# Score sums of a gated layer kept in two PSUM tiles, with V's columns cleared by ScalarE

## The reference, cut to what matters

```python
Q = einsum('bshd,hde->bshe', layernorm(x), Wh)
K = einsum('bshd,hde->bshe', ctx, Wh)
V = einsum('bshd,hde->bshe', ctx, Wh)
scores = einsum('bshe,bthe->bhst', Q, K) / sqrt(128)
A = maximum(abs((scores * Dn).sum(axis=0)), 1.0)   # one A for the whole batch
O = einsum('hst,bthe->bshe', A, V)
Y = (O - mean) / sqrt(var + eps) * gamma + beta
x = x + tanh(g0) * ((relu(layernorm(x) @ wg) * Y) @ wo)
```

## Time and profile before

| | |
|---|---|
| time, median of 3 runs | 1507.49 us (1504.81 to 1509.27) |
| the profiled execution's own time | 1504.33 us |
| its span | 1502.5 us |
| TensorE busy | 1483.4 us (99%) |
| VectorE busy | 1096.5 us (73%) |
| ScalarE busy | 698.3 us (46%) |
| GpSimd busy | 744.9 us (50%) |
| mean granted TensorE clock | 0.999 |

### The profile page before, as it was taken

How to read it: one execution, slowest core, us unless ns; L and a number is a source line. 1 busy time by engine, 2 the same in 40 slices (tenths; PEclk the granted TensorE clock), 3 DMA queues, 4 the chain that set the end, 5 groups by cost and what they waited for, 6 DMA issues and landing times.

```text
span 1502.5 us, 20476 instructions
## 1 busy us (share of the span) xinstructions
PE 1483.4 (99%) x7182; PEld 1246.3 (83%) x7182; DVE 1096.5 (73%) x1592; ACT 698.3 (46%) x1094; POOL 744.9 (50%) x774
## 2 busy tenths in 40 slices
PE   7999999999999999999999999999999999999998
PEld 5888888888888887888888888888888888888887
DVE  7776778788578687677686763777778778778672
ACT  4444434445565545555646534344344344443442
POOL 5556666771445553545645534137237137237236
PEclk9999999999999999999999999999999999999999
DMA  6888788876778779888898785373473562562422
GB/s 225 301 262 271 262 282 282 255 234 221 250 229 279 237 221 305 261 246 282 240 288 281 209 240 158 116 217 105 125 212 107 144 208 95 146 199 93 149 90 85
DMA packets 237753, 316.05 MB, mean 210 GB/s; under 512 B 135696, under 2 KB 161680, under 8 KB 237456
## 3 DMA queue, kind: packets, MB, share of 16 engines
q1 hardware_dynamic: 237648, 314.71, 66.0%
HBM read 210.32 MB, written 117.31 MB: 218 GB/s over the span
## 4 chain that ended last, share of the span: by engine, by line
PE 86%; DVE 4%; DMA 3%; POOL 2%; SPq 1%; ACT 1%; issue 1%; DVEq 0%; ACTq 0%; POOLq 0%
PE ps L1785 33%; PE po L1785 10%; PE pyb L1664 8%; PE ptb L1785 7%; PE pyb L1785 7%; PE ps L1699 5%; PE po L1664 5%; PE pyb L1769 3%; PE ptb L1769 3%; PE pyb L1773 2%; PE ptb L1773 1%; PE ptb L1669 1%; PE ps L1664 1%; DMA wy_scratch<-misc 1%; POOL reg L1536 1%
## 5 line engine op out<-in xcount | busy, mean ns | idle before, releaser
L1785 PE MATMUL ps<-op,wbuf 128*128 128x512 f32 x880 | 217.3, 389 | 0.0
L1563 POOL TENSOR_TENSOR p5b<-p5b,p1b 128x512 f32<-128x512 f32 x55 | 71.3, 1296 | 268.6 <-ACT p5b L797 268.6
L1491 POOL TENSOR_SCALAR rs<-mv 128x1 f32<-128x1 f32 (+1 forms) x132 | 48.4, 367 | 295.7 <-DVE mv L1116 157.3
L1785 PEld LDWEIGHTS ps<-op,wbuf 128*128 128x128 f32 x880 | 165.2, 188 | 34.3
L1574 POOL TENSOR_TENSOR hsp<-hall,hsp 128x640 fp32r<-128x640 f32 (+2 forms) x90 | 172.3, 1931 | 42.3 <-ACT hsp L824 42.3
L1664 PE MATMUL pyb<-reg,xreg 128*128 128x512 f32 x708 | 177.9, 398 | 2.2 <-DVE reg L1005 2.2
L1785 PE MATMUL po<-op,wbuf 128*128 128x512 f32 x660 | 168.3, 389 | 0.0
L1664 PEld LDWEIGHTS pyb<-reg,xreg 128*128 128x128 f32 x708 | 129.8, 189 | 28.4 <-DVE reg L1005 2.4
L1785 PEld LDWEIGHTS po<-op,wbuf 128*128 128x128 f32 x660 | 123.9, 188 | 25.7
L1785 PE MATMUL ps<-reg,gate 128*128 128x512 f32 x528 | 130.8, 390 | 0.0
L1785 PE MATMUL ps<-reg,up 128*128 128x512 f32 x528 | 130.7, 390 | 0.0
(11 more groups left out here) (154 smaller groups left out, 2937.7 us busy)
## 6 DMA issues: line engine op xcount, KB each, us to landing
wbuf<-ws_scratch SPq DMA_DIRECT2D x55, 896.0 KB, 4.7
xr<-in_x SPq DMA_DIRECT2D x62, 512.0 KB, 5.4
raw<-in_ctx_t SPq DMA_DIRECT2D x32, 512.0 KB, 4.6
w_scratch<-tmp SPq DMA_DIRECT2D x64, 256.0 KB, 5.1
v_scratch<-tmp SPq DMA_DIRECT2D x64, 256.0 KB, 4.5
raw<-v_scratch SPq DMA_DIRECT2D x32, 512.0 KB, 6.5
x_scratch<-xr SPq DMA_DIRECT2D x32, 512.0 KB, 5.6
xr<-x_scratch SPq DMA_DIRECT2D x32, 512.0 KB, 5.8
```

Source lines behind the costliest of these rows:

```text
L1491: e.tensor_scalar(dst, var, eps, None, ALU.add).then_inc(s["eps"])
L1563: e.tensor_tensor(p5b[n % 2][:, :], p5b[n % 2][:, :], p1b[n % 2][:, :], ALU.add).then_inc(s["p15"])
L1785: last = e.matmul(dst, l, r, start=(k == 0 and i == 0), stop=(k == n - 1 and i == 1), skip_group_check=sums)
```

## The change

TensorE now adds the score columns of the tiles itself: even tiles in `ps[0]`, odd tiles in `ps[1]`. No matmul of `v` sets `start` any more, so each adds to what the bank holds. The V columns of a tile must then be zero before the tile two later comes, and ScalarE sees to that: `v_out` has a second instruction (L684 of the new kernel) that copies a zero, read from one column `nil`, over the V columns. It waits for the copy before it. There are 62 of these. Both `ps` tiles are cleared whole by VectorE at the start (two memsets of 128x1024). All 64 `v_acc` are gone; after the last tile VectorE copies the sum of `ps[0]`, adds that of `ps[1]`, and multiplies by the mask.

```diff
-        acc = misc[:, 0:512].rearrange("p (h n) -> p h n", h=4)
+        nil = sb("nil", [128, 1])
                 e.copy(tmp[:, 2 + t % 2, :].rearrange("p (h n) -> p h n", h=4), ps[t % 2][:, :, 0, :]).then_inc(s["vev"])
+                if t + 2 < B:
+                    p.wait_ge("vev", t + 1)
+                    p.wait_ge("ones", 4)
+                    e.copy(ps[t % 2][:, :, 0, :], nil[:, 0:1].to_broadcast([128, 4, 128])).then_inc(s["vz"])
...
-            def v_acc(t):
-                p.wait_ge("vev", t + 1)
-                if t:
-                    p.wait_ge("acc", t)
-                    e.tensor_tensor(acc, acc, ps[t % 2][:, :, 1, :], ALU.add).then_inc(s["acc"])
-                else:
-                    e.tensor_copy(acc, ps[0][:, :, 1, :]).then_inc(s["acc"])
...
+            e.memset(ps[0][:, :, :, :], 0).then_inc(s["clear"])
             stats(0)
...
             wg_lo(0)
+            p.wait_ge("tbxe", 3)
+            e.memset(ps[1][:, :, :, :], 0).then_inc(s["clear"])
             xt_lo(3)
...
-                v_acc(4 * g)
-                v_acc(4 * g + 1)
...
-            p.wait_ge("acc", B)
+            p.wait_ge("v", B)
...
-            e.tensor_tensor(xr[:, 7, :].rearrange("p (h n) -> p h n", h=4), acc,
-                            xr[:, 3, :].rearrange("p (h n) -> p h n", h=4), ALU.mult).then_inc(s["ad"])
+            both = xr[:, 7, :].rearrange("p (h n) -> p h n", h=4)
+            p.wait_ge("vev", B - 1)
+            e.tensor_copy(both, ps[0][:, :, 1, :]).then_inc(s["ss"])
+            p.wait_ge("ss", 1)
+            p.wait_ge("vev", B)
+            e.tensor_tensor(both, both, ps[1][:, :, 1, :], ALU.add).then_inc(s["ss"])
+            p.wait_ge("ss", 2)
+            e.tensor_tensor(xr[:, 7, :], xr[:, 7, :], xr[:, 3, :], ALU.mult).then_inc(s["ad"])
...
+            e.memset(nil[:, :], 0).then_inc(s["ones"])
...
                 if t >= 2:
-                    p.wait_ge("vev", t - 1)
-                    p.wait_ge("acc", t - 1)
+                    p.wait_ge("vz", t - 1)
+                else:
+                    p.wait_ge("clear", t + 1)
...
-                                        wh_and_z(q, h, b), start=(n == 0), stop=(n == 2))
+                                        wh_and_z(q, h, b), start=False, stop=(n == 2), skip_group_check=True)
```

More of the change, by code:

```diff
@@ L18 @@
     + ["scr0", "scr1", "wld0", "wld1"]
-    + ["ones", "eps", "rs", "rs2", "cthi", "ctlo", "sadd", "p15"]
+    + ["ones", "clear", "eps", "rs", "rs2", "cthi", "ctlo", "sadd", "p15"]
     + ["wq0", "wq1", "wq2", "sst", "gst"]
@@ L24 @@
     + ["tbxh", "tbwh", "tb2h", "Ghi", "whhi", "cthf", "zhi", "wghi", "vev", "wev", "vhi", "wohi", "tg", "si", "hhi"]
-    + ["st", "mv", "xn", "tbxe", "tbwe", "tb2e", "Glo", "whlo", "ctlf", "zlo", "wglo", "acc", "and", "low", "lowm"]
+    + ["st", "mv", "xn", "tbxe", "tbwe", "tb2e", "Glo", "whlo", "ctlf", "zlo", "wglo", "vz", "ss", "and", "low", "lowm"]
     + ["ad", "ahi", "alo", "flag", "vlo", "wolo", "nm", "nr", "aff", "wm", "wylo", "wyb", "x2b", "x1", "st2", "mv2", "nm2", "xn2", "ds", "h", "hlo"]
@@ L1293, in _ @@
             stats(7)
-            v_acc(0)
             norm(6)
             xt_lo(5)
-            v_acc(1)
             norm(7)
@@ L1301, in _ @@
             xt_lo(7)
-            v_acc(2)
             norm(8)
             stats(9)
-            v_acc(3)
             for g in range(1, NG):
@@ L1321, in _ @@
                     v_lo(0)
-                v_acc(4 * g)
-                v_acc(4 * g + 1)
                 if not more:
                     low_sums(3, 3)
-                    v_acc(4 * g + 2)
-                    v_acc(4 * g + 3)
                     break
@@ L1708, in w @@
                 elif t == LATE + 1:
-                    p.wait_ge("acc", B - 1)
+                    p.wait_ge("ss", 1)
                     p.wait_ge("vev", B - 1)
```

## The result

| | before | after |
|---|---|---|
| median of 20 runs each, side by side | 1504.28 us | 1509.64 us |
| lowest and highest | 1502.57, 1509.27 | 1507.60, 1513.29 |
| ratio, 95% interval | | 1.0034 [1.0027, 1.0042] |
| profiled execution: own time, span | 1504.33, 1502.5 | 1508.85, 1507.1 |

The change costs 0.34%, or 5.1 us; between the two profiled executions it is 4.5 us. The forecast was 1510.6 us, but it is near to 1509.64 for a reason that must be said: it stood on the 1507.49 us of three runs, and the 20 runs of the kernel before, those three among them, have their median at 1504.28. That the forecast lies so near is in part luck. The difference is what the prediction worked out, and there it said +3.1 where +4.5 to +5.1 came. The prediction gave 65% to a change of less than 0.3%; the measured 0.34% is just beyond that bound, and its interval reaches to both sides of it.

A forecast was written before the change was run, and what follows sets the result against it. TensorE was taken to bound the kernel. Boundary terms 1.8 + 0.05 + 0.5 + 0.8 - 0.1 = 3.05, say 3.1 us, with start and end 0, took 1507.49 to 1510.6 us; range 1506 to 1515.5.

The forecast's parts named there:

- What bounds the kernel: TensorE, busy 99% of the span; VectorE's 44 us could save at most 2.2 us plus a few at the start.
- The matmuls: The 768 matmuls of 128x256, median 283 ns: all of them adding counted 0; v(62) starts 0.1 us sooner.
- The clear: 62 ScalarE instructions zeroing 512 columns of ps, taken at 0.59 us each, behind the copy and ahead of xt_hi.
- The shift of xt_lo: At tile boundaries VectorE's xt_lo starts 0.5 us later, since clear and xt_hi stand in a row on ScalarE.
- Place by place: Boundary costs: four without margin 0.45 us each, one 0.05, group 15's z 0.5, xt(62) 0.8, ordinary ones nothing.
- The fifth boundary: Near 212.6 us, counted at 0 because a norm there waits for GpSimd longer than the shift; other end 0.5.
- the lighter VectorE counts: Rival: VectorE's queue runs ahead, saving 2.2 us at its waits and 1 at the start, to 1504.3 us; 4%.
- The start: ps1's memset of 1.1 us delays the first product, 0.3 us left; missing additions give 0.4 back; net 0, -0.5 to +1.1.
- The end: After the last tile, the copy of ps0 runs beside ScalarE's last copy of V; 0 us.
- The clear is dear: Rival: a clear of 0.8 us on ScalarE's queue costs 5.0 us, 1512.5; at 1.05 us about 8, 1515.5; 24%.
- The margins give way: Rival: lost time at one boundary is another's margin, or the clear is shorter; 1508.5 us; 12%.
- The clock: Rival at the start: TensorE's longer stand may bring another 1.2 GHz stretch, 1.7 us at most; no chance given.

The follow-up runs named there:

- e4: The kernel before without its 64 VectorE additions and without clears, so the sum over the batch is left out; 1503.36 us, ratio 0.9990.
- e3: The kernel before, additions and matmuls kept, with ScalarE also writing 512 zeros 62 times to an unused place in SBUF; 1508.39 us, ratio 1.0025.
- e1: The changed kernel with 55 of the 62 clears issued after the xt_hi that follows their copy; 1505.21 us, ratio to before 0.9997.
- c0_after: The changed kernel run once more, beside the experiments; 1509.85 us, ratio to before 1.0031.
- e8: The changed kernel with V's columns cleared by VectorE where its additions stood, ScalarE's queue as before; 1503.71 us, ratio to before 0.9997.
- e11: The changed kernel with ps[1] cleared at the start by two ScalarE copies instead of VectorE's memset; 1508.86 us, ratio to before 1.0026.
- e10: The changed kernel with the load of wo issued ahead of the store of w tile 57 on SyncE's queue; 1508.94 us, ratio to before 1.0026.
- e6: The changed kernel with the edits of e1, e10 and e11 together; 1502.87 us, ratio to before 0.9988.
- e9: The changed kernel with the edits of e8 and e11 together; 1502.63 us, ratio to before 0.9989.
- e5: The changed kernel with each ScalarE clear issued twice; 1522.18 us, ratio to before 1.0108.

## Why the prediction was right, and what it mis-sized

**What bounds the kernel.** Right. TensorE's path sets the time, and 44 us off VectorE are worth 1.5 us (e4), within what the idle time of 180 to 345 us and the start had allowed.

**The matmuls: 0.** Right: 274, 283 and 387 ns. At v(62) 0.2 us came where I had 0.1.

**The clear: 0.59 us.** Right (0.589), by the nearest row of the same engine, opcode and count of columns. ScalarE's zeros to PSUM took 0.589 us, its copy of V to SBUF 0.587 us, and the zeros that e3 writes to SBUF as bf16 0.617 us. The Trainium skill (page "ScalarE: Activation LUTs", section "Step-by-step: what each stage is for") has ScalarE faster to PSUM than to SBUF. Of these three the two with the same source, `nil`, agree with it, but by 0.028 us only; with a clear of 0.5 us the sum would have been 0.6 us further off.

**The shift of xt_lo: 0.5.** Measured 1.76 - 1.23 = 0.53. What follows a clear on ScalarE starts 0.52 to 0.53 us behind the clear's start (98.32 to 98.84), where I had taken the 0.48 that it is behind a copy. Less the margin of 0.05 that makes 0.48 at a boundary; they cost 0.51 to 0.56, and xt(62), with two such gaps, 0.90 where I had 0.8. The six places together are 3.56 us where the sum had 3.1.

**Place by place.** The four boundaries, group 15's z and xt(62) are where the steps stand, and e3 and e1 show the cause from both sides: with only ScalarE's zeros all steps come, with the clears behind xt_hi nearly all go. One place I had wrong by a little: 0.22 us were lost at 235.3, at a boundary whose margin I had not looked at (c0_after and e3 lose 0.2 there too, e1, e4 and e8 nothing). The fifth boundary (212.6) I counted at 0, and between 207 and 214.4 us TensorE in fact gained 0.35 us. In the kernel before the z ahead of it waited for xt_lo:

```profile
207.44 1.67 PE L1664 MATMUL po<-reg,xreg 128*128 128x512 f32 x6 [0.28 <-DVE reg L1005]
```

and in after it does not. This looks like the rival "the lighter VectorE counts", but it isn't: e3, with all of VectorE's additions, gains the same 0.44 us at this z. It is the copy of V that had waited for a store in the trace of before. So the gain hid some 0.4 us of what the clears cost, and that the sum came as near as 3.05 to 3.43 is in part luck.

**The start: net 0.** It came to +0.20, and to +0.46 in c0_after. VectorE ahead of the first product, before (its next instruction is the xt_lo at 13.36 in the earlier trace rows):

```profile
12.76 0.68 DVE L1017 TENSOR_TENSOR xreg<-tmp,xreg 128x512 fp32r<-128x512 f32 x1
```

and in after:

```profile
12.84 0.68 DVE L1021 TENSOR_TENSOR xreg<-tmp,xreg 128x512 fp32r<-128x512 f32 x1
...
13.73 0.91 DVE L1270 MEMSET ps<- 128x1024 f32 x1 [0.21 <-issue]
...
14.56 0.67 DVE L1009 TENSOR_TENSOR reg<-pyb,reg 128x512 fp32r<-128x512 f32 x1
```

The record gives the memset 0.91 us, but from the instruction ahead of it to the one behind it is 1.72 us where it was 0.60: it costs 1.12, near the 1.1 that I took and the estimate of 1.07 beside it, and the first product moved by 1.1. At 22.24 us 0.57 were left where I had worked out 0.3; the norm that had run for 1.54 us now took 0.75, and that gave 0.53 back, where I had 0.4. The two parts are now known apart: the missing additions give about 0.9 to 1.2 us (e11, e4) and the memset takes about 1.1 (after against e11). The net was right, but as a sum of two larger terms, one of which was to be had for nothing.

**The end: 0.** This is the step that failed. I followed ScalarE's last copy of V, and it does run as said; what I didn't follow was the other instruction behind the last clears, w_out(57), and who waits for that: SyncE's store, then the load of wo queued behind the store, then ScalarE's casts, then two copies of w, then TensorE. It cost 0.65 us here, 0.29 in c0_after and 1.0 in e11 (e10: 0 with the load moved). The prediction had followed what waits behind a clear for xt_hi only.

**The last 0.4 us** between 355 us and the end stay open. Against the one profiled execution of the kernel before, the stage from 355 us on is longer by 0.4 (after, e11), about 1 (e4, e6, e9, e10), 1.8 (c0_after, e3), 2.1 (e1) and 2.6 us (e5), and by nothing in e8. e4 has no clears and no sums over the batch, and its stage behind the tiles runs the instructions of the changed kernel; so part of this is that execution being a quick one there, and one profile of each can't give this term to better than 1 or 2 us. That also covers the distance between 4.5 us by the profiles and 5.1 us by the ratio.

**The rivals.** "The clear is dear" falls with 0.589 us; its sum of 5.0 us is near the measured 5.1 by accident, since the clear of 0.8 us that it needs isn't there. That a longer hold of the queue costs more than in proportion, e5 does show. "The margins give way" isn't seen: the 0.35 us between 207 and 214 us are there without clears too. The clock: TensorE's granted clock in the window of the earlier trace rows and in the next of equal length, in after:

```profile
14.60:18.00 3.40, 2.72 (x7) 2.17 (x8) 3.37 (x8) 0.76 (x3) 1.03 (x2) 0.67 0.35 139
18.00:21.40 3.40, 3.40 (x14) 2.70 (x13) 2.44 (x3) 2.60 (x6) 2.94 (x4) 0.83 0.00 0
```

The two windows together lose as much as before (granted 0.50 and 1.00 there, 0.67 and 0.83 here): the stretch at 1.2 GHz behind the stand moved with the first product, and no other came. Its length isn't the same in every execution, though. While the granted clock is 0.50 the matmuls of 512 columns start 0.43 us apart, otherwise 0.23; before and after have seven such gaps of 0.43, c0_after has eleven and e8 ten (their clock column stands at 1.00 there, so that the column alone would have missed them). The four more of c0_after are 0.8 us: it is 1.38 us behind at 22.24, after 0.57. At 34 us 0.26 of this difference is left.

## What to carry to other kernels

When an instruction is put on an in-order queue, list everything that stands behind it, DMAs and loads queued behind those too, and give each a margin; work taken off an engine that waits is worth only the waits it ended (here 1.5 of 44 us). Put such an instruction behind the one that the critical chain needs, not ahead of it: the same 62 clears cost 5 us ahead of xt_hi, and with 55 of them behind it nothing that could be measured. A cost that is hidden by margins isn't linear: the first 0.6 us cost 5 us, the second 11.

## What the runs showed of the hardware that I had not expected

- The record of VectorE's memset is shorter than the time that the memset takes from its queue. For fp32 zeros in PSUM it has 0.91 us for 128x1024 and 0.485 us for 128x512, but the instructions around it move apart by 1.11 to 1.12 us (six kernels) and 0.54 us (e8). ScalarE's clear of 512 columns has a record of 0.589 us, and the next instruction starts 0.52 us behind it. So neither engine is the quicker one for clearing PSUM here; what decides is who waits behind the clear. The cost of an instruction on a queue is read from the starts around it.
- A lead at the start is kept and a delay there is mostly lost: e11's 0.89 us were still 0.75 at 172 us, while of the changed kernel's 1.09 us at the first product 0.20 were left at 34 us. From 40 to 180 us TensorE has no idle time (140.00 of 140 us busy), so there is nothing in which a delay could be made up.
